# A projection piece moved between the two score pairs of an attention turn

## The reference

```
q, k, v = heads(binlinear(layernorm(x), W, b))      # weights: mean(|W|) per row times sign(W)
att = softmax(q @ k.T * Dh**-0.5)
x = x + layernorm(binlinear(att @ v, Wp, bp))
z = layernorm(x)
h = silu(tlin(z, w1)) * tlin(z, w2)                 # ternary weights with a scale per row
h = gelu(tlin(h, h1)); h = gelu(tlin(h, h2))        # 1024 wide
x = x + layernorm(tlin(h, w3))
```

## Time and profile before

| | us |
|---|---|
| median of 3 runs | 1269.48 (1268.64 to 1273.58) |
| profiled execution, its own time | 1268.93 |
| its span, first to last instruction | 1267.2 |
| exponentials of the attention stage, first start to last end | 47.9 to about 581 |
| ScalarE in that stretch: busy with them, idle | 477.4, 68.1 |

### The profile page before, as it was taken

The page is one execution under the profiler, slowest core; times in us unless marked ns, Lnnn a source line. Parts: engine busy times, 40 slices in busy tenths (PEclk is TensorE's granted clock), DMA queues, the critical chain, the costliest instruction groups (busy, mean ns, idle before and its releaser), DMA issues.

```text
span 1267.2 us, 17503 instructions
## 1 busy us (share of the span) xinstructions
PE 1192.1 (94%) x6705; PEld 726.3 (57%) x6705; DVE 632.8 (50%) x1163; ACT 728.1 (57%) x871; POOL 77.8 (6%) x77
## 2 busy tenths in 40 slices
PE   5499989999899989998999999999999999999998
PEld 4132322323232322225888888888888888888886
DVE  7243424453353321533556647656566376565624
ACT  6589888888989899996224234243242342432421
POOL 6011101111011100000000000000000000000000
PEclk9699999999999999999999999999999999999999
DMA  5967667887786778502000101001001011010000
GB/s 195 238 155 208 175 144 163 218 182 147 169 191 130 164 147 158 80 25 59 15 19 24 43 1 34 34 1 48 19 20 48 1 34 34 1 34 1 17 1 18
DMA packets 53336, 107.55 MB, mean 85 GB/s; under 512 B 6784, under 2 KB 23552, under 8 KB 53244
## 3 DMA queue, kind: packets, MB, share of 16 engines
q1 hardware_dynamic: 52956, 105.93, 35.4%
q10 hardware_dynamic: 288, 0.39, 0.2%
HBM read 71.94 MB, written 45.88 MB: 93 GB/s over the span
## 4 chain that ended last, share of the span: by engine, by line
PE 53%; DVE 1%; issue 0%; ACT 0%; POOLq 0%; DVEq 0%
PE ffn_ps L1603 24%; PE ffn_ps L1602 23%; PE ffn_ps L1631 2%; PE ffn_ps L1630 2%; PE side_ps L1586 1%; PE side_ps L1595 0%; DVE ln_stats L1831 0%; DVE zn L1842 0%; DVE zn L1839 0%; DVE zn L1829 0%; PE ffn_ps L1644 0%; PE ffn_ps L1645 0%; DVE ln_mean_var L1833 0%; ACT hid L1716 0%; DVE h_lo L1856 0%
## 5 line engine op out<-in xcount | busy, mean ns | idle before, releaser
L1203 ACT ACTIVATE probs<-s_ps 128x1024 f32<-128x1024 f32 x512 | 477.4, 1052 | 68.1 <-PE s_ps L1047 67.9
L1603 PE MATMUL ffn_ps<-h_lo,W 128*128 128x512 f32 x1024 | 405.9, 396 | 0.0
L1602 PE MATMUL ffn_ps<-h_hi,W 128*128 128x512 f32 x1024 | 403.0, 394 | 0.0
L1059 PE MATMUL y_ps<-probs,v_st 128*17 128x512 f32 x2048 | 272.5, 604 | 34.0 <-ACT probs L1203 17.6
L1603 PEld LDWEIGHTS ffn_ps<-h_lo,W 128*128 128x128 f32 x1024 | 192.0, 188 | 47.5
L1716 ACT ACTIVATE hid<-ffn_ps,scales 128x512 f32<-128x512 f32 x128 | 81.1, 686 | 240.0 <-PE ffn_ps L1603 235.0
L1602 PEld LDWEIGHTS ffn_ps<-h_hi,W 128*128 128x128 f32 x1024 | 191.9, 187 | 45.7
L1047 PE MATMUL s_ps<-q_st,k_st 50*128 50x512 f32 x1024 | 190.0, 449 | 19.8 <-issue 15.8
L1047 PEld LDWEIGHTS s_ps<-q_st,k_st 50*128 50x128 f32 x1024 | 77.5, 187 | 199.5 <-ACT probs L1203 162.9
L1862 DVE CAST h_hi<-hid 128x512 fp32r<-128x512 f32 x128 | 53.5, 418 | 192.7 <-ACT hid L1716 192.3
L1856 DVE TENSOR_TENSOR h_lo<-hid,h_hi 128x512 fp32r<-128x512 f32 x192 | 130.2, 685 | 1.1
(11 more groups left out here) (172 smaller groups left out, 918.6 us busy)
## 6 DMA issues: line engine op xcount, KB each, us to landing
k_st<-qk_scr SPq DMA_DIRECT2D x90, 128.0 KB, 6.6
q_st<-qk_scr SPq DMA_DIRECT2D x90, 128.0 KB, 7.1
w_scr<-ffn_w SPq DMA_DIRECT2D x16, 704.0 KB, 7.3
W<-w_scr SPq DMA_DIRECT2D x16, 704.0 KB, 6.1
y_scr<-y_sb SPq DMA_DIRECT2D x32, 256.0 KB, 2.5
qk_scr<-y SPq DMA_DIRECT2D x24, 256.0 KB, 2.5
qk_scr<-sums SPq DMA_DIRECT2D x24, 256.0 KB, 4.0
v_st<-v_scr SPq DMA_DIRECT2D x16, 272.0 KB, 10.5
```

What stands on the lines that cost most here:

```text
L1059: i = pe.matmul(y_ps[32 * j:32 * j + VCOLS, :], v_st[g % 2][:, s, VCOLS * j:VCOLS * (j + 1)], probs[turn % 2][j // 2][:, j % 2, :], start= ...
L1203: act.activation(probs[turn % 2][pp][:, :, :], s_ps[a % 3][:, :, :], ACT.Exp, scale=SCALE).then_inc(probs_ready, 1)
L1602: pe.matmul(bank_of(t)[:, :], w, hi[:, k, :].bitcast(form), start=(k == 0), stop=False)
L1603: mm = pe.matmul(bank_of(t)[:, :], w, lo[:, k, :].bitcast(form), start=False, stop=last)
```

## The change

The helper `scores` now issues one pair, not two, and the piece of turn t - 1 goes between the two pairs of turn t. In the kernel before, it stood directly ahead of the first of these pairs. The order of a turn is: first pair of t, piece of t - 1, second pair of t, values of t - 1. No instruction is added or removed, and the orders of the other engines stay as they are. Turn 63 has no piece, so that none is lost at a batch's end.

```diff
-            def scores(turn):
+            def scores(turn, pp):
...
-                if s == 0 and tb == 0:
+                if s == 0 and tb == 0 and pp == 0:
                     pe.wait_ge(loaded[u], loads_of(g))
                     pe.wait_ge(m_loaded[u], 16 * 2 * (g // 2 + 1))
-                for pp in range(PAIRS):
-                    a = PAIRS * turn + pp
-                    if a >= 3:
-                        pe.wait_ge(probs_ready, a - 2)
...
+                a = PAIRS * turn + pp
+                if a >= 3:
+                    pe.wait_ge(probs_ready, a - 2)
...
+            def between_scores(b, t):
+
+                if b + 1 < BATCH:
+                    projected(b + 1, t)
+                else:
+                    prepared(t)
+
...
-                    scores(turn)
+                    scores(turn, 0)
+                    if t:
+                        between_scores(b, t - 1)
+                    scores(turn, 1)
                     if turn:
                         pv(turn - 1)
-                    if b + 1 < BATCH:
-                        projected(b + 1, t)
-                    else:
-                        prepared(t)
             pv(TURNS - 1)
```

More of the change, by code:

```diff
@@ L1037, in scores @@
                 u = g % 2
-                if s == 0 and tb == 0:
+                if s == 0 and tb == 0 and pp == 0:
                     pe.wait_ge(loaded[u], loads_of(g))
                     pe.wait_ge(m_loaded[u], 16 * 2 * (g // 2 + 1))
-                for pp in range(PAIRS):
-                    a = PAIRS * turn + pp
-                    if a >= 3:
-                        pe.wait_ge(probs_ready, a - 2)
[L1045 to L1049, removed]
+                a = PAIRS * turn + pp
+                if a >= 3:
+                    pe.wait_ge(probs_ready, a - 2)
+                for hh in range(2):
+                    rows = slice(hh * HALF, hh * HALF + STACK_M)
+                    i = pe.matmul(s_ps[a % 3][:, hh, :], k_st[u][rows, pp, s * P:(s + 1) * P],
+                                  q_st[u][rows, pp, tb * BLK:(tb + 1) * BLK], start=True, stop=True)
+                i.then_inc(scored, 1)
             def pv(turn):
```

## The result

The changed kernel takes 1273.14 us in the median of 12 executions (1270.82 to 1278.13), the kernel before 1268.41 in the median of 12. The ratio is 1.0039, interval 1.0025 to 1.0054: 4.7 us slower, clear of the noise and inside what was called "same" (under 0.5%). A second set of 12 gave 1273.37 and 1.0029 (1.0016 to 1.0041).

A forecast was written before the change was run, and what follows sets the result against it. ScalarE waits for TensorE, itself nearly a bound at 1.64 of 1.83 us a turn. Terms sum to +1.3 a batch, +3.9 over three, 0 for the last: 1268.93 to 1272.8 us, range 1263 to 1277.

The forecast's parts named there:

- first pair to piece; second pair to values: TensorE's start-to-start slots in a q/k turn after the change: 0.44 at the high end, and 0.43 for the lone pair.
- seven q/k pieces: Lateness of exponentials from a batch's q/k pieces: 1.07 against 1.04 each, +0.03 for each of seven, +0.2 a batch.
- q/k piece of turn 47 with v piece of turn 49: Around turn 48, whose values wait for VectorE's copy: split and copy move 0.44 later, exponential 10.74 against 10.27, +0.47.
- three other v pieces: Lateness from a batch's other v pieces: 0.99 after against 1.06 before, -0.07 each, -0.2 a batch.
- transposes, two windows: Transposes in two turns in a row: lateness 1.15 after against 0.91 before, +0.25 a window, +0.5 a batch.
- sums of squares: Two sum-of-squares pieces a batch: lateness 0.91 after against 0.77 before, together +0.3.
- tiny pieces: The tiny pieces put between the pairs: 0, hidden behind or equal in both kernels.
- The unknown step: TensorE's step from first score pair to piece: between 0.34 with its load hidden and 0.44 as a full switch.
- The high end: First pair to piece as full switch, pause 0.10 and load 0.11: 0.44, piece's first slot 0.33; 1272.8 us, chance 0.55.
- rivals 1 and 2: First pair to piece: load paid without pause, 1266.4, chance 0.15; or load hidden too, 1262.2, chance 0.12.
- The late copy: VectorE's copy awaited by turn 48's values comes 0.44 later, costing 0.47; TensorE's wait there grows from 1.20 to 1.51.
- Rival 3: The clock falls at turn 48's longer wait of 1.51: three more falls cost 3.6, giving 1276.4; chance 0.13.

The follow-up runs named there:

- uncut: Against the kernel before: both score pairs first, then the piece of the turn before, then the values; ratio 0.9965, median 1265.16 us.
- qk_between: Against the kernel before: only the q/k pieces moved between the pairs, all others left behind the values; ratio 1.0007.
- tiny_old: The changed kernel with the two tiny pieces of the second window put back behind the values; ratio 1.0020 to the kernel before.
- rest_between: Against the kernel before: all pieces except the q/k pieces moved between the pairs; ratio 1.0022.
- tiny_only: Against the kernel before: only the two tiny pieces of the second window moved between the pairs; ratio 1.0012.
- copy_first: The uncut order, offsets as they were, with VectorE taking the copy of y ahead of the piece of the turn before; ratio 1.0000 to the kernel before.

## Why the prediction was right

The forecast was +3.9 on the profiled execution. It measured +2.7, and +4.7 in the medians. That the median of 1273.14 lies 0.3 from the forecast of 1272.8 is luck: the order cost less than forecast (2.5 at equal clock, 2.8 in the spans), and the clock, put at nothing, added about 1.2 by the difference of 0.0013 in its mean. The parts, with one of them mis-sized (second batch, lateness by starts of exponentials, after minus before):

| term | predicted | measured |
|---|---|---|
| first pair to piece; second pair to values | 0.44; 0.43 | 0.43; 0.42 |
| seven q/k pieces | +0.2 | -0.24 |
| q/k piece of turn 47 with v piece of turn 49 | +0.47 | +0.44 |
| three other v pieces | -0.2 | -0.27 |
| transposes, two windows | +0.5 | +0.45 |
| sums of squares | +0.3 | +0.36 |
| tiny pieces | 0 | +0.05 |
| a batch | +1.3 | +0.8 |

- *The unknown step*, first pair to piece, is a full switch. The high end was the right choice; rivals 1 and 2 are out by the rows of a q/k turn and by the 0.20 between uncut and the changed order.
- *The mis-sized term* is the q/k pieces. The first of each window was 0.1 cheaper (0.97 against 1.07), and so was the one of turn 41 (1.12 against 1.22); the others fitted (1.09 to 1.11 against 1.08 to 1.10). The chain started each piece from a ScalarE that is just on time; behind the transposes and behind a copy it isn't (this reason is read from where the cheaper pieces stand; no run tested it). The exponential behind the lone pair was ready after 0.54, not 0.60, and the next gave those 0.06 back (0.56 late for 0.50).
- *The late copy* was right in place and price: 0.47 for 0.44. As a wait on TensorE it was priced at 1.51 and shows 1.43.
- *The other batches*: the first was unchanged (137.54 and 137.46), since the fall of the clock at its turn 56 wasn't there after; the third grew by 1.9 (133.43 to 135.36), since a fall was now at its start; the last was 0.2 shorter, and the wait ahead of it 0.5 longer. Each of the two profiled executions has two falls in the stage, so that they nearly cancel in the 2.8.
- *Rival 3* was wrong as put and right in kind. None of the twelve waits of 1.42 or 1.43 at turn 48 in the four profiled executions that have them (the changed kernel's two, qk_between, tiny_old) was followed by a fall; the three of 1.86 in the uncut order all were. Yet the changed kernel has a lower mean clock, and more falls per execution are the likely part of the step from the 2.8 of the spans to the 4.7 of the medians. Its profiles have one at the start of the third batch, at 322.8 and 326.7 us, and so have rest_between, tiny_only and tiny_old (324.3, 324.8, 326.0); the kernel before has none there. TensorE's wait for the shift's load at that start was 1.42 to 1.96 in the five and 1.47 in the kernel before, so its length alone doesn't tell. Of the 25 falls within the attention stage in the twelve profiles, 15 lie at a batch's start, seven at turn 56 and only three at turn 48. Why a wait at a batch's start ends in a fall in one order and not in the other stays open.
- *The skill's rule.* By the Trainium skill ("TensorE: Matmul & The Clock Gate", the mechanism of row and column tiling) a load can go to the background weight buffer under products in flight. The rows agree within a piece (0.11 behind the load before) and not across a change of shape, where 0.25 without loads stands ahead of the piece. That the shape is the reason is argued from which steps pause; no run changed the shape alone.

## What to carry to other kernels

When two engines are both within some ten per cent of their bound (here 1.64 us of 1.83 a turn), moving work between two waits doesn't hide it: count what the move adds to the fuller engine, first of all products of one shape that it splits apart. Here the same q/k piece 0.23 us later, behind both pairs, was the step from 1.0029 to 0.9965, and a piece kept away from the turn in which VectorE owes a copy was worth another 0.5 to 0.7%. Look for what an engine owes next in its own order before placing work on it, and compare starts, not idle sums, when the number of waits changes. Look at the queues as well: in copy_first the larger loss was a load at each batch's start, behind a store that stood behind another transfer.

## What the runs showed of the hardware

- TensorE: where 50-row pairs and 128-row products alternate, each change costs a pause of 0.10 and leaves the 0.11 of the load uncovered, in both directions (0.43 and 0.42 against 0.34 and 0.32; the piece's first slot 0.34 against 0.23).
- The clock: of TensorE's waits of 1.20 to 1.43 us at turn 48, 21 in seven profiled executions, none was followed by a fall to 0.50. All five of 1.86 (turns 48 and 56) were; at turn 56 one of 1.77 and both of 2.42 and 2.43 were, one of 1.87 and three of the five of 2.16 or 2.17 weren't. At batch starts, waits of 1.41, 1.42 and 1.51 had a fall beside them, and two of 1.82 had none. A fall lasts 3.4 us (6.8 in five places of the stage); third batches with one at their start are 1.1 to 1.2 longer than the second batch of the same execution.
- The shift's store of 64 KB, issued 1.0 us behind a part of W on the same queue, had its load issued 6.5 us later (5.0 to 6.9 over the profiles), once it had landed, and a batch's first scores waited for that load.
- A whole batch repeats to 0.02 us between executions when no fall lies in it; the spread of 5 to 10 us over 12 or more executions goes mostly with the mean granted clock, some 0.9 us for each 0.001.
